# Attention with 16-wide heads: both scores of a turn on the same half, one placing of the maxima, and loops written out

## The chip, the cores and the metric

The kernel runs on one core of a Trainium2 chip. The metric is the device time of one execution in microseconds (us), the median over runs. TensorE (PE in the rows) multiplies, VectorE is DVE, ScalarE is ACT, GpSimd is POOL, SyncE (SP) issues most transfers.

## What is computed

Four layers on 16 sequences of 128 tokens, width 256; each layer is self-attention, cross-attention and a feed-forward part, each followed by a residual and a layer norm. Four of these twelve parts run through one function, `attention16`: the cross-attentions of layers 1, 2 and 3 (stages x1, x2, x3) and the self-attention of layer 3 (stage a3). Cut to what matters:

```python
def attention(x, ctx):                       # 16 heads of 16, 128 queries, 128 keys
    q, k, v = split(x @ Wq), split(ctx @ Wk), split(ctx @ Wv)
    scores = einsum('bhqd,bhkd->bhqk', q, k) / 4   # x1: q, k rotated by position first
    probs = softmax(scores)                  # x2: masked; a3: scores + log(penalty)
    return einsum('bhqk,bhkd->bhqd', probs, v)     # then @ Wo + bo (not in a3)
x = layernorm(x + attention(x, ctx))
```

The penalties of a3 are made in stage ao2, which also adds the outputs of layer 2's experts:

```python
g = sigmoid(h @ Wg + bg)
res = (1 - Zi) * max(1 - Zi - Zj, 0) + Zi * min(1 - Zi + Zj, 1)
scope = clip(126 ** (1 - g) + 2 - abs_ij, 1e-32, 1)
```

## The kernel before

**A turn.** `attention16` handles one sequence in a turn, 16 turns (n = 0 to 15). Queries lie in `qx` and keys in `kx`, [128, 4, 128] each: a row group of 32 rows holds two heads of 16 rows, and of the four slots (c) each keeps one head of every group. Where the other head's rows would be, there is one row that is -1 in `kx` and is to hold the query's maximum in `qx`, so that a product over 32 rows gives the score less the maximum. A half is two of the four row groups (rows 0 to 63, or 64 to 127); 8 of the 16 heads belong to each.

**The steps for a half.** TensorE computes the scores with queries as rows (`score`, L2094, 8 matmuls of 32 x 128 x 128 in float32), VectorE takes the maximum over keys (`maximum`, L2323), TensorE transposes the maxima (`maxima`, L2154), VectorE adds them to their rows of `qx` (`put_maxima`, L2329, four instructions on 64 partitions, 128 elements), TensorE computes the scores again, shifted and with keys as rows (`shifted_score`, L2099, 8 matmuls), ScalarE takes the exponential (L2226). Then come the values (`attend_values`) and the sums of the columns (`attend_sums`), both L2124, VectorE's reciprocal and product (`normalise`, L2380, L2383), the output matrix (`output`, L2146), residual and layer norm (`residual`, `spread`, `scaled`; the root on GpSimd, L1990), and the transposed result goes back to `XT` (`turn_back`).

**Which scores are paired.** The order of a turn is written out by hand. `score_halves` issues two kinds together, matmul by matmul: the scores of half 0 of turn n with the shifted scores of half 1 of turn n - 1, later the scores of half 1 of turn n with the shifted scores of half 0 of the same turn:

```python
for c in range(SLOTS16):
    for j in range(NH):
        done = score(half, j, c, w)
        if shifted:
            last = shifted_score(other, j, c, tw)
```

Here `other = 1 - half`. So four row groups take part in a block. Each half has its own tile `pS[half]` of PSUM, which holds first the scores and then the shifted ones, and its own tile `mx[half]` of maxima. Each float32 matmul is two records in the trace (8 matmuls show as x16), and of one matmul they follow each other in the program.

**The order.** On TensorE in x1 and a3: block 0, turn back, projections of turn n + 1, maxima 0, block 1, (turned keys,) output of n - 2, values of n - 1, maxima 1, sums. In x2 and x3 (`kv`: keys and values were projected in an earlier stage) the output comes between maxima 0 and block 1. VectorE: maximum 0, put 0, maximum 1, residual and spread of n - 2, put 1, scaled, normalise of n - 1; in a3 also `weigh`, the product with the penalties, 1.2 us for each half. The first four and the last two turns are written out, ten run in a hardware loop of two turns. Before a stage's first matmul TensorE waits until GpSimd has cleared `V` and `mx` (L1949). GpSimd also copies the sequence's keys to `kvs` for the values' matmul in x1 and a3.

**Stage ao2.** `add_outputs_and_penalties` loads the experts' biases with 16 small transfers behind a clearing of their tile, all at the stage's start; TensorE waits for them before the first `bias`. The function `least`, three instructions on GpSimd, makes min(1 - Zi + Zj, 1) Zi for groups 0 to 2 of 4, VectorE makes it for the last. VectorE's order is sums 0, 1, 2, penalty 0, sums 3, penalties 1, 2, 3.

## Time and profile before

| | |
|---|---|
| median of 3 runs | 3023.47 us (3021.82 to 3034.4) |
| the profiled execution | 3028.75 us, its span 3026.8 us, granted clock 0.906 of full |
| stage x1, from the first clearing to the last copy to `XT` | 235.05 us |
| stage x2 | 200.48 us |
| stage a3 | 226.03 us |
| stage x3 | 170.38 us |
| stage ao2 | 75.01 us |

Busy over the whole span: TensorE 2443.6 us (81%), VectorE 1523.6 (50%), ScalarE 874.6 (29%), GpSimd 690.0 (23%). These are means over stages with different limits, so each of the five stages is read by itself. Busy TensorE is the time in which at least one matmul is under way, and matmuls overlap.

### The profile page before, as it was taken

Reading aid. Unit: us, or ns where it says so; the run is one execution under the profiler, and the core shown is the slowest. Engines: PE = TensorE matmul, PEld = TensorE weight load, DVE = VectorE, ACT = ScalarE, POOL = GpSimd, SP = SyncE. Lnnn points to the kernel's source line nnn. Section 1 sums busy time; section 2 is a strip of 40 time slices with the busy share of each in tenths; the row PEclk is TensorE's granted clock in tenths of the full one; section 3 lists DMA queues with packets and bytes.
Section 4 is the critical chain, followed back from the end, with each engine's and each line's share of the span. In section 5 each row is a group of like instructions: output and inputs, shape, how many; then the busy total and the mean of one; then the engine's idle time right before and its main releaser. Section 6 shows DMA issues by size and latency. Waiting matters only on the chain. (4 is left out here: it accounts for less than half of the span.)

```text
span 3026.8 us, 55542 instructions
## 1 busy us (share of the span) xinstructions
PE 2443.6 (81%) x20565; PEld 1911.5 (63%) x20565; DVE 1523.6 (50%) x3278; ACT 874.6 (29%) x1558; POOL 690.0 (23%) x1052
## 2 busy tenths in 40 slices
PE   7879998579788799999799878549867757589990
PEld 3857776334567465899688655338556646479990
DVE  3256665775387531111467557541268858721115
ACT  1123333554234211011222244203244435212220
POOL 1932222331133100122112101113221111123331
PEclk8889999889899999999899989769889969889995
DMA  8010000000200000888200020116200000179982
GB/s 324 28 52 1 0 0 6 25 0 1 78 2 0 29 1 0 318 315 315 90 15 0 4 68 0 34 54 183 65 1 1 0 4 1 36 267 323 327 294 85
DMA packets 163394, 253.06 MB, mean 84 GB/s; under 512 B 17744, under 2 KB 124496, under 8 KB 163024
## 3 DMA queue, kind: packets, MB, share of 16 engines
q1 hardware_dynamic: 154064, 230.46, 21.9%
q0 software_dynamic: 9216, 21.06, 2.6%
q8 instruction: 74, 1.21, 0.2%
q14 instruction: 40, 0.33, 0.0%
HBM read 220.36 MB, written 31.13 MB: 83 GB/s over the span
## 5 line engine op out<-in xcount | busy, mean ns | idle before, releaser
L3274 PE MATMUL te_pU<-te_xsT,te_wu 128*128 128x128 f32 x1952 | 236.2, 278 | 1.5 <-DVE te_xsT L3354 1.5
L3274 PEld LDWEIGHTS te_pU<-te_xsT,te_wu 128*128 128x128 f32 x1952 | 233.7, 195 | 5.4 <-issue 2.3
L3295 PE MATMUL te_pY<-te_wd,te_hT 128*128 128x256 f32 x976 | 220.8, 379 | 0.0
L3295 PEld LDWEIGHTS te_pY<-te_wd,te_hT 128*128 128x128 f32 x976 | 180.7, 190 | 22.0
L2094 PE MATMUL x_pS<-x_kx,x_qx 32*128 32x128 f32 x1536 | 120.2, 296 | 62.2 <-issue 34.4
L2323 DVE TENSOR_REDUCE x_mx<-x_pS 128x8 f32<-128x1024 f32 x96 | 117.5, 1224 | 92.4 <-PE x_pS L2094 91.7
L2094 PEld LDWEIGHTS x_pS<-x_kx,x_qx 32*128 32x128 f32 x1536 | 102.9, 199 | 95.8 <-issue 95.8
L2226 ACT ACTIVATE x_Pr<-x_pS 128x1024 f32<-128x1024 f32 x96 | 98.3, 1024 | 161.1 <-PE x_pS L2099 161.1
L1117 PE MATMUL x_pB<-early,x_xlT 128*128 128x384 f32 x384 | 137.5, 502 | 4.7 <-DVE x_qn L1344 3.0
L2329 DVE SCALAR_TENSOR_TENSOR x_qx<-x_pX,place,x_qx 64x128 f32<-64x128 f32 x384 | 109.7, 347 | 23.1 <-PE x_pX L2154 19.7
L2099 PE MATMUL x_pS<-x_qx,x_kx 32*128 32x128 f32 x1536 | 118.3, 294 | 0.7 <-DVE x_qx L2329 0.7
L3315 ACT ACTIVATE te_hT<-te_pU 128x512 f32<-128x512 f32 x78 | 46.6, 597 | 243.2 <-PE te_pU L3274 243.2
L3333 DVE COPY te_ys<-te_pY 128x256 f32<-128x256 f32 x61 | 25.9, 425 | 162.8 <-PE te_pY L3295 162.8
L3328 DVE TENSOR_TENSOR te_hT<-te_pU,te_sg 128x512 f32<-128x512 f32 x44 | 30.4, 692 | 150.4 <-ACT te_sg L3313 150.4
L1117 PEld LDWEIGHTS x_pB<-early,x_xlT 128*128 128x128 f32 x384 | 71.1, 195 | 47.7 <-issue 5.2
L2099 PEld LDWEIGHTS x_pS<-x_qx,x_kx 32*128 32x128 f32 x1536 | 99.4, 196 | 1.7 <-DVE x_qx L2329 1.2
L3313 ACT ACTIVATE te_sg<-te_pG 128x512 f32<-128x512 f32 x44 | 26.3, 597 | 252.4 <-PE te_pG L3274 252.4
L3330 DVE COPY te_xsT<-te_pT 128x256 f32<-128x256 f32 x61 | 25.7, 421 | 135.2 <-PE te_pT L3268 135.2
L1990 POOL TENSOR_TENSOR x_rstd<-x_ve,mhalf 128x1 f32<-128x1 f32 x48 | 26.4, 551 | 292.0 <-DVE x_ve L2370 292.0
L3274 PE MATMUL te_pG<-te_xsT,te_wg 128*128 128x128 f32 x704 | 87.1, 278 | 0.0
L2036 PE MATMUL x_pq<-XT,early 128*128 (+1 forms) x512 | 75.4, 302 | 12.4 <-POOL x_mx L1949 12.4
L2380 DVE RECIPROCAL x_R<-x_pO 128x256 f32<-128x256 f32 x48 | 84.3, 1757 | 1.4
(625 smaller groups left out, 5757.8 us busy)
## 6 DMA issues: line engine op xcount, KB each, us to landing
te_wu<-in_L_ffn_w_upT SPq DMA_DIRECT2D x39, 1024.0 KB, 5.4
te_wd<-in_L_ffn_w_downT SPq DMA_DIRECT2D x39, 1024.0 KB, 5.6
te_wu<-in_L_ffn_up SPq DMA_DIRECT2D x22, 1024.0 KB, 4.8
te_wg<-in_L_ffn_gate SPq DMA_DIRECT2D x22, 1024.0 KB, 6.9
te_wd<-in_L_ffn_down SPq DMA_DIRECT2D x22, 1024.0 KB, 7.6
moe_first<-in_L_ffn_W SPq DMA_DIRECT2D x8, 1024.0 KB, 8.7
ao_got<-ys_slots SPq DMA_DIRECT2D x12, 512.0 KB, 6.1
xs_slots<-zeros SPq DMA_DIRECT2D x1, 5120.0 KB, 23.5
```

The source lines that it names most:

```text
L1117: ins = pe.matmul(pB[:, n, 0:HALF], xlT[t][:, src + k, :], w[:, k, bass.ts(n, HALF)], start=(k == 0), stop=(k == KD - 1))
L2036: ins = pe.matmul(out[:, t, :], ws[t // KD][:, k, bass.ts(t % KD, P)], src[:, k, bass.ts(b, P)], start=(k == 0), stop=(k == KD - 1))
L2094: return pe.matmul(pS[half][:, j, c, :], qx[w][g, c, :], kx[w][g, c, :], start=mask is None, stop=mask is None or c == SLOTS16 - 1)
L2099: return pe.matmul(pS[half][:, j, c, :], kx[w][g, c, :], qx[w][g, c, :], start=mask is None, stop=mask is None or c == SLOTS16 - 1)
L2226: ins = act.activation(Pr[w][half][:], pS[half][:], ACT.Exp, scale=SCALE)
L2323: dve.tensor_reduce(out, pS[half][:], AX.X, ALU.max).then_inc(mx_ready[half], 1)
L2329: ins = dve.scalar_tensor_tensor(out=qx[w][g, c, :], in0=pX[g, 2 + half, :], scalar=place[g, c:c + 1], in1=qx[w][g, c, :], op0=ALU.mult, o ...
L2380: dve.reciprocal(R[:], pO[:, 1, :, :]).then_inc(o_inverted, 1)
L3274: ins = pe.matmul(out[g][:, m, :], w[:, k, bass.ts(PER * g + m, P)], xsT[:, k, :], start=(k == 0), stop=(k == KD - 1))
L3295: ins = pe.matmul(pY[u][:, 0, :], hT[:, k, :], wd[u][:, k, :], start=(k == 0), stop=(k == KH - 1))
L3315: act.activation(hT[:, PER * g:PER * (g + 1), :], pU[g][:], act_fn).then_inc(h_done, 1)
L3328: dve.tensor_tensor(hT[:, PER * g:PER * (g + 1), :], pU[g][:], sg[g][:], ALU.mult).then_inc(h_done, 1)
```

## The change

- **Pairing.** `scores(n, half)` issues the scores of that half of turn n into one tile `pR` and the shifted scores of the same half of turn n - 1 into another, `pT`. Both are used for half 0 and again for half 1, so block 1 waits for the maximum and the exponential of block 0.
- **Maxima.** Both halves write one tile `mx` [128, 2, 128]; TensorE makes two transposes in one go after block 1; `put_maxima` is two instructions on 128 partitions, 256 elements each. The constants `others`, `minus` and `place` have two columns, so that `key` is two instructions (in a3 still four).
- **Depth.** Work of earlier turns is one turn later than before: the output is of turn n - 3 (a3: n - 4), turning back of n - 4 (n - 5); in a3 the values are those of n - 2 (`LAG` = 2). `qx` and `kx` have four buffers, `V` three (a3: four), `oT` two.
- **Loops.** All turns are written out; the `hold` increments go. TensorE no longer waits for the clearing; ScalarE does for `V` and VectorE for `mx`. `kvs` and its copies go.
- **ao2.** The biases' tile is kept from earlier: cleared by a transfer at the start of x2, loaded by 16 small transfers in the experts' stage behind the second expert's weights. `least` goes, VectorE does its two instructions in every group, in the order sums 0, sums 1, penalty 0, sums 2, penalty 1, sums 3, penalties 2, 3. TensorE begins with bias 0; the last group's keys are made after the first logits.

```diff
@@ attention16
+        LAG = 2 if penalty is not None else 1
+        TURNS = range(-1, NB + LAG + 3)
-        pS = [s.ps(f"pS{i}", [P, NH, SLOTS16, P]) for i in range(2)]
+        pR, pT = s.ps("pR", [P, NH, SLOTS16, P]), s.ps("pT", [P, NH, SLOTS16, P])
@@ tensor
+            def scores(n, half):
+                if mask is not None:
+                    if live(n):
+                        masks(pR, mask[0], n)
+                    if live(n - 1):
+                        masks(pT, mask[1], n - 1)
                 for c in range(SLOTS16):
                     for j in range(NH):
-                        done = score(half, j, c, w)
-                        if shifted:
-                            last = shifted_score(other, j, c, tw)
+                        if live(n):
+                            done = score(half, j, c, n)
+                        if live(n - 1):
+                            last = shifted_score(half, j, c, n - 1)
+            for n in TURNS:
+                if live(n):
+                    since(pe, q_stored, n)
+                    since(pe, k_stored, n)
+                    since(pe, mx_ready[1], n - 1)
+                if live(n - 1):
+                    since(pe, m_stored, n - 1)
+                    since(pe, e_done[1], n - 2)
+                scores(n, 0)
+                if rope and live(n + 1):
+                    projections(n + 1)
+                if live(n - LAG - 3):
+                    turn_back(n - LAG - 3)
+                if own and live(n - LAG - 2):
+                    output(n - LAG - 2, n)
+                if kv and live(n + 1):
+                    projections(n + 1)
+                if live(n):
+                    since(pe, mx_ready[0], n)
+                if live(n - 1):
+                    since(pe, e_done[0], n - 1)
+                scores(n, 1)
+                if own and live(n + 1):
+                    projections(n + 1)
+                if rope and live(n + 1):
                     turned_keys(n + 1)
+                if not own and live(n - LAG - 2):
+                    output(n - LAG - 2, n + 1)
+                if not kv and live(n):
+                    maxima(n)
+                if live(n - LAG):
+                    attend_values(n - LAG)
+                if kv and live(n):
+                    maxima(n)
+                if live(n - LAG):
+                    attend_sums(n - LAG)
@@ vector
+            def put_maxima(b):
+                since(dve, m_ready, b)
+                for i in range(PAIR):
+                    here = qx[b % 4][:, KD * i:KD * (i + 1), :]
+                    ins = dve.scalar_tensor_tensor(out=here, in0=pX[:, 2:4, :], scalar=place[:, i:i + 1], in1=here,
+                                                   op0=ALU.mult, op1=ALU.add)
+                ins.then_inc(m_stored, 1)
+            for n in TURNS:
+                if live(n):
+                    maximum(n, 0)
+                if own and live(n - LAG - 2):
+                    residual(n - LAG - 2)
+                if rope and live(n + 1):
+                    rotate(n + 1, q_ready, bqc, bqc2, rq, q_turned, q_summed)
+                if live(n - LAG - 1):
+                    normalise(n - LAG - 1)
+                if live(n):
+                    maximum(n, 1)
+                if rope and live(n + 1):
+                    rotate(n + 1, k_ready, bkc, bkc2, rk, k_turned, k_summed)
+                if not own and live(n - LAG - 2):
+                    residual(n - LAG - 2)
+                if live(n):
+                    put_maxima(n)
+                if live(n - LAG - 2):
+                    spread(n - LAG - 2)
+                if penalty is not None and live(n - 1):
+                    weigh(n - 1, 0)
+                    weigh(n - 1, 1)
+                if live(n - LAG - 2):
+                    scaled(n - LAG - 2)
@@ stage ao2
-            core.x3.wait(pe)
-            kv.make_keys(pe, 0)
             pe.wait_ge(wT_stored, 1)
-            pe.wait_ge(loaded, 16 * NG * G)
+            pe.wait_ge(lists.biases_loaded, 16 * NG * G)
             bias(0)
-            for g in range(1, NG):
+            core.x3.wait(pe)
+            for g in range(NG - 1):
                 kv.make_keys(pe, g)
```

## Rows read from the trace of the kernel before

**Rows 1.** The page, its first line: the whole span
```profile
span 3026.8 us, 55542 instructions
```

**Rows 2.** Windows by stage: x1, x2, a3, x3, ao2 (busy us of each engine, clock)
```profile
797.69:1032.74 235.05, 180.66 (x2752) 152.93 (x2752) 167.78 (x400) 83.42 (x161) 67.26 (x116) 0.95 0.08 26
1736.73:1937.21 200.48, 157.20 (x2432) 107.56 (x2432) 133.63 (x272) 80.23 (x160) 27.53 (x52) 0.93 0.09 27
2227.77:2453.80 226.03, 162.94 (x2464) 131.23 (x2464) 170.90 (x309) 90.98 (x192) 41.59 (x85) 0.84 0.00 1
2456.62:2627.00 170.38, 124.69 (x2304) 98.62 (x2304) 131.79 (x272) 80.34 (x160) 27.51 (x52) 0.91 0.01 2
2151.31:2226.32 75.01, 60.59 (x225) 36.34 (x225) 47.54 (x87) 32.35 (x49) 22.61 (x18) 0.89 0.10 30
```

**Rows 3.** The same, steady turns: 11 of x1, 10 of x2, 12 of a3, 12 of x3
```profile
866.46:1009.22 142.76, 115.86 (x1885) 98.31 (x1883) 114.78 (x277) 56.40 (x112) 44.96 (x76) 1.00 0.00 1
1794.58:1904.06 109.48, 90.93 (x1521) 62.92 (x1522) 83.34 (x171) 49.89 (x100) 16.39 (x30) 1.00 0.00 1
2268.78:2418.91 150.13, 113.99 (x1849) 91.48 (x1850) 126.53 (x228) 68.06 (x144) 28.21 (x59) 0.91 0.00 1
2489.40:2599.57 110.17, 85.95 (x1736) 68.16 (x1734) 98.43 (x205) 60.01 (x121) 19.65 (x36) 1.00 0.00 1
```

**Rows 4.** Groups of stage x1 (count, busy us, mean ns, idle before)
```profile
L2323 DVE TENSOR_REDUCE x_mx<-x_pS 128x8 f32<-128x1024 f32 x32 | 39.1, 1223 | 28.7 <-PE x_pS L2094 28.6
...
L2329 DVE SCALAR_TENSOR_TENSOR x_qx<-x_pX,place,x_qx 64x128 f32<-64x128 f32 x128 | 36.5, 346 | 1.2 <-PE x_pX L2154 0.6
```

**Rows 5.** Timeline of TensorE, first turn of x1 (start us, us)
```profile
810.29 1.16 PE L2094 MATMUL x_pS<-x_kx,x_qx 32*128 32x128 f32 x16 [3.75 <-issue]
811.38 3.56 PE L2036 MATMUL x_pq<-XT,early 128*128 128x128 f32 x16
...
817.30 0.34 PE L2094 MATMUL x_pS<-x_kx,x_qx 32*128 32x128 f32 x1 [1.25 <-issue]
817.31 0.37 PE L2099 MATMUL x_pS<-x_qx,x_kx 32*128 32x128 f32 x1
817.31 0.37 PE L2094 MATMUL x_pS<-x_kx,x_qx 32*128 32x128 f32 x1
817.32 0.37 PE L2099 MATMUL x_pS<-x_qx,x_kx 32*128 32x128 f32 x1
...
818.40 2.05 PE L2036 MATMUL x_pq<-CT,early 128*128 128x128 f32 x16
```

**Rows 6.** Timeline of all engines, one turn of x3
```profile
2545.78 0.33 PE L2154 MATMUL x_pX<-ident,x_mx 128*128 128x128 f32 x1 [0.36 <-DVE x_mx L2323]
...
2546.04 1.08 PE L2124 MATMUL x_pO<-x_Pr,ones_half 128*32 128x128 f32 x32
2546.15 1.17 DVE L2329 SCALAR_TENSOR_TENSOR x_qx<-x_pX,place,x_qx 64x128 f32<-64x128 f32 x4
...
2547.35 1.76 DVE L2380 RECIPROCAL x_R<-x_pO 128x256 f32<-128x256 f32 x1
...
2547.57 0.34 PE L2094 MATMUL x_pS<-x_kx,x_qx 32*128 32x128 f32 x1 [0.45 <-DVE x_qx L2329]
...
2548.82 1.02 ACT L2226 ACTIVATE x_Pr<-x_pS 128x1024 f32<-128x1024 f32 x1 [1.07 <-PE x_pS L2099]
...
2550.92 1.04 PE L2146 MATMUL x_pk<-early,x_oT 128*128 128x256 f32 x4
```

**Rows 7.** Timeline of TensorE, start of x3
```profile
2458.00 2.05 PE L2036 MATMUL x_pq<-XT,early 128*128 128x128 f32 x8 [4.69 <-POOL x_mx L1949]
```

**Rows 8.** Timeline of stage ao2, three places
```profile
2158.97 0.66 PE L4043 MATMUL ao_pb<-ao_biases,ao_WT 32*128 32x512 f32 x1 [1.32 <-DMA ao_biases<-in_L_ffn_b]
...
2167.62 1.38 DVE L4140 TENSOR_SCALAR ao_xn<-ao_r,ao_mv,ao_rstd 128x256 f32<-128x256 f32 x4 [1.17 <-POOL ao_rstd L4011]
...
2194.73 2.47 DVE L4140 TENSOR_SCALAR ao_xn<-ao_r,ao_mv,ao_rstd 128x256 f32<-128x256 f32 x4 [1.14 <-POOL ao_rstd L4011]
```

More of the change, by code:

```diff
@@ L2038, in project, with value @@
                 return ins
-            def value():
+            def value(b):
                 for k in range(KD):
-                    ins = pe.matmul(pv, kvs[:, k, :], wv[:, k, :], start=(k == 0), stop=(k == KD - 1))
-                return ins
-            def y_free(b):
-                if not (isinstance(b, int) and b <= 1):
-                    pe.wait_ge(y_used, b - 1)
-            def projections(b, first=False):
+                    ins = pe.matmul(pv, KV[:, k, bass.ts(b, P)], wv[:, k, :], start=(k == 0), stop=(k == KD - 1))
+                ins.then_inc(v_ready, 1)
@@ L2079, in turned_keys, with masks @@
             def turned_keys(b):
-                pe.wait_ge(q_turned, b + 1)
-                hold(pe, core)
+                since(pe, q_turned, b)
                 project(pq, (wk, wk2), KV, b).then_inc(k_ready, 1)
-            def masks(half, table, b):
+            def masks(out, table, b):
                 for j in range(NH):
-                    pe.matmul(pS[half][:, j, :, :], core.identb[:],
+                    pe.matmul(out[:, j, :, :], core.identb[:],
                               table[:, b, :].unsqueeze(1).to_broadcast([P, SLOTS16, P]), start=True, stop=False)
@@ L2136, in attend_sums @@
-            def attend_sums(w):
-                columns(1, lambda h, i: ones_half[:, i, :], w).then_inc(o_ready, 1)
-            def output(b, ahead):
-                pe.wait_ge(oT_ready, b + 2)
-                pe.wait_ge(y_used, b + 2)
-                if not kv and ahead:
-                    pe.wait_ge(v_copied if rope else k_stored, b + ahead)
+                                            Pr[b % 2][g // NH][:, g % NH, KD * (1 - i) + t, :], start=(i == 0),
+                                            stop=(i == PAIR - 1))
@@ L2192, in _ @@
-            projections(0, first=True)
-            if rope:
-                turned_keys(0)
-            every_turn(pe, turn)
-            LAST = NB - 1
-            pe.wait_ge(m_stored[1], NB)
-            if mask is not None:
-                masks(1, mask[1], LAST)
-            for c in range(SLOTS16):
-                for j in range(NH):
-                    ins = shifted_score(1, j, c, 1)
-            ins.then_inc(t_ready[1], 1)
-            turn_back(LAST - 2)
-            output(LAST - 1, 0)
@@ L2298, in _ @@
-            query(0, 0)
-            value(0, 0)
-            key(0, 0)
-            every_turn(act, turn)
-            exponentials(NB - 1, 1, 1)
-            for b in range(NB - 3, NB):
-                turn_back(b)
+            for n in TURNS:
+                if live(n - 1):
+                    exponentials(n - 1, 0)
+                if live(n - LAG - 3):
+                    turn_back(n - LAG - 3)
+                if rope and live(n + 1):
+                    value(n + 1)
+                if not own and live(n + 1):
+                    query(n + 1)
+                if live(n - 1):
+                    exponentials(n - 1, 1)
+                if own and live(n + 1):
+                    query(n + 1)
+                    value(n + 1)
+                if live(n + 1):
+                    key(n + 1)
+                if kv and live(n + 1):
+                    value(n + 1)
@@ L2411, in _ @@
-            if rope:
-                turn_queries(0, first=True)
-                turn_keys(0, first=True)
-            every_turn(dve, turn)
-            residual(NB - 2)
-            spread(NB - 2)
-            if penalty is not None:
-                weigh(NB - 1, 1, 1)
-            scaled(NB - 2)
-            normalise(NB - 1)
-            residual(NB - 1)
-            spread(NB - 1)
-            scaled(NB - 1)
+                since(dve, y_ready, b - 2)
+                dve.tensor_tensor(oT[b % 2][:], pO[:, 0, :, :], R[:], ALU.mult).then_inc(oT_ready, 1)
@@ L3945, in _, with add_outputs_and_penalties @@
                 steps.end()
-def add_outputs_and_penalties(core, a, name, W, b2, got, keys, values, weight):
+def add_outputs_and_penalties(core, name, W, lists, keys, values, weight):
     BASE = float(np.log(P - 2.0))
@@ L4089, in _ @@
             act.copy(WT[:], pw[:, 0, :]).then_inc(wT_stored, 1)
[L4090 removed]
+            for g in range(NG - 1):
                 kv.store_keys(act, g)
@@ L4160, in _ @@
             sums(0)
-            sums(1)
-            sums(2)
-            penalty(0)
-            sums(3)
-            penalty(1)
-            penalty(2)
-            penalty(3)
+            for g in range(1, NG):
+                sums(g)
+                penalty(g - 1)
+            penalty(NG - 1)
 def expert_weights(core, keep, name):
@@ L4205, in layer2 @@
         list_experts(core, a, "te2", ACT.Gelu_apprx_tanh, lists, after=[core.x3])
-        add_outputs_and_penalties(core, a, "ao2", W, "L2_ffn_b2", lists.outputs, core.keys3, spare, core.pen.weight)
+        add_outputs_and_penalties(core, "ao2", W, lists, core.keys3, spare, core.pen.weight)
 def layer3(core, a, spare):
```

509 lines of the change are left out of this document (177 added, 332 removed).

## The prediction

> **What bounds the kernel now.** I read the page for the whole span [rows 1], cut it by stage [rows 2], and then took from each of the four attention stages a stretch of steady turns [rows 3]. The reader is to see there that no engine is full. A turn takes 142.76 / 11 = 12.98 us in x1, 109.48 / 10 = 10.95 in x2, 150.13 / 12 = 12.51 in a3 and 110.17 / 12 = 9.18 in x3. VectorE is busy for 10.4, 8.3, 10.5 and 8.2 us of it, TensorE for 10.5, 9.1, 9.5 and 7.2. Neither has much room, and the rest is waits of one for the other: VectorE waits for the scores before its maximum 28.7 us in x1 [rows 4], TensorE for the maxima put in their place [rows 6]. So a change can gain by VectorE's work, or by unlocking the chain, and it loses where it adds to TensorE's.
>
> **The block of scores.** This is the term on which the sum hangs. In x1's first turn a block is alone, without shifted scores: 16 records (8 matmuls) on two row groups, and the next matmul starts 811.38 - 810.29 = 1.09 us later. The following block has 32 records on four row groups and takes 818.40 - 817.30 = 1.10 us [rows 5]. Twice the work cost nothing, because it fell on other row groups: in both cases a row group gets 8 records, so a record costs about 0.11 us of its group, and about 0.2 us are start and switch. The new pairing puts the scores and the shifted scores of the same half together, so 32 records fall on two row groups: 16 x 0.11 + 0.2 = about 1.98 us, 0.88 us more per block, 1.76 us per turn. The bounds: 1.10 us, if something other than the row group (the PSUM bank, of which four are still used) sets the pace, and 2.84 us, if the two groups overlap only where the program goes from one to the other. In that case the 32 records have 24 gaps of 0.11 us, since four records in a row now belong to one group. I take 1.98, since the four first records start at 817.30 to 817.32 on four groups [rows 5], although the second record of each matmul stands between them in the program: a blocked group doesn't hold the others.
>
> The Trainium skill, in TensorE: Matmul & The Clock Gate, Part 3, says the reverse, that matmuls start strictly in program order and only weight loads are pulled ahead. By it the block would be the 2.84 us; the trace of before speaks against it, in the same four records.
>
> **VectorE's part.** `put_maxima` has 8 instructions of 0.346 us per turn [rows 4], 1.17 us busy for each half [rows 6]. The new ones have 256 elements on all partitions. The reduction of 1,024 elements takes 1.223 us and this one of 128 takes 0.346 [rows 4], so an element costs about 0.98 ns and one with 256 takes about 0.47; two take 0.9 us. That frees 1.4 us per turn. Bounds for the two: 0.7 us (each as short as now) and 1.4 (each as two of the old).
>
> **x3, by its new chain.** Block 0 starts at 0 and ends at 1.98. The maximum starts 0.1 later and takes 1.22, and TensorE starts 0.25 us after VectorE's last instruction (put from 2546.15 to 2547.32, block at 2547.57 [rows 6]): block 1 from 3.6 to 5.6. Projections and turning back lie under the maximum, VectorE's reciprocal (1.76 us [rows 6]) and product under block 1. Then the exponential of block 1 starts 0.15 later and takes 1.02 [rows 6]; the output matrix (1.04 us) lies under it. The values of turn n - 1 need that exponential and stand ahead of the transposes in the program: from 6.9 to 7.9 (as the sums, 1.08 us with its tail [rows 6]). Two transposes reach VectorE at 8.4 (one takes 0.37 from 2545.78 to 2546.15 [rows 6]), put ends at 9.3, and the next block 0 starts at 9.6. The sums of the columns lie under put. VectorE's spread, a wait for GpSimd's root, which nothing on VectorE covers in this order, and scaled lie under the next block 0; without that cover the wait would be paid in each turn. So 9.6 us against 9.18: the chain was to be loosened, but the wider blocks stand twice in it. 16 x 0.4 = 6.5 us lost.
>
> **x2** adds the mask matmuls, 10.95 - 9.18 = 1.77 us per turn at present, and they stand in the chain as before: 11.4 against 10.95, 7 us lost.
>
> **x1.** TensorE has 10.5 us per turn at full clock [rows 3], and 1.76 more make 12.3. VectorE has 10.4 - 1.4 = 9.0, and the path from the turned keys over GpSimd and ScalarE has its two instructions of `key` in place of four. I take TensorE as the bound, as the busier one: 12.3 against 12.98, 16 x 0.7 = 11 us gained.
>
> **a3.** Here VectorE also weighs, so the freed work and the second turn of lag count. VectorE needs 10.5 - 1.4 = 9.1 us [rows 3]; in the new order it waits before put for the transposes, which stand behind the projections of the next turn (16 records of 0.11 us and 4 of twice the width, 2.6 us); normalise and the rest cover some 1.5 us of it, which leaves an estimated 1.1 us, and 0.4 us of handovers: 10.6. TensorE has 9.5 us at a clock of 0.91 and gets 1.8 more, 11.3, or less if the clock rises with the load. I take 11.0 against 12.51: 16 x 1.5 = 24 us gained.
>
> **Starts and ends.** TensorE now starts without GpSimd's clearing, on which x3's first matmul waited [rows 7]: 1.4 us per stage. The end of a stage is longer by about 3 us, since the last blocks come one after the other through single tiles and the last two turns' layer norms queue with one turn more of depth. 6 us lost in four stages. The loops written out and `kvs` I leave at nothing: branches and copies lie beside the longer work, and without that cover they'd be tenths of a microsecond per turn. More instructions to fetch are priced by no row; the transfer engines' share is 0.00 in the steady turns [rows 3], so there is room for them.
>
> **ao2.** TensorE waits for the biases until 2158.97, 7.7 us into the stage [rows 2, 8]. With them there, bias 0 starts at about 2152, and the first layer norm begins when the experts' outputs land, about 5.5 us earlier. The 16 transfers move to the experts' queue ahead of a wait for a whole expert, so they delay nothing. Without `least` beside it the same instructions take 1.38 us, with it 2.47 [rows 8], so VectorE gets 1.5 us more of work per group and loses as much of slowing down. The last group's keys, too, go behind the first turning back, which takes some 3 us from TensorE's path ahead of it. A group then needs sums and penalty on VectorE one after the other, as it does at present from group 2 on. So the stage ends at least the 5.5 us earlier, at most these, the keys' 3 and twice 2 us of slowing down (12.5); I take 10.
>
> **The sum.** x1 -11, x2 +7, x3 +6.5, a3 -24, starts and ends +6, ao2 -10: about -26 us. From the profiled execution's 3028.75 us that is 3003; it lies 5.3 us above the median of the runs, 3023.47, so I predict 2998 us for the median.
>
> **Rivals.**
> - *Matmuls in strict order* (the other side). Each block costs 2.84 us, 0.86 more, twice in the chain of each of 64 turns: +110 us, 3108 us. It decides against the change from 1.98 + 0.2 us per block on. For it: four records of one group in a row are new, and no row shows such a block. Against it: [rows 5]. 12%.
> - *Exposed waits.* The chain of a turn now has single tiles between TensorE, VectorE and ScalarE, and if each of the handovers costs 0.05 to 0.1 us more than I have read, a turn is 0.35 us longer: 22 us, 3020. For it: x2 and x3 are chains without slack. 20%.
> - *The row group isn't the pace.* Blocks stay at 1.1 us; then x1 has 10.6, x3 7.8, x2 9.7 and a3 10.5, another 92 us: 2906 us. Against it: a record costs 0.11 us of its group in both blocks of [rows 5]. 4%.
> - *My forecast* as it stands, 2975 to 3012 us: 60%. A larger gain in a3 and ao2 (put cheaper, the clock up), 2960 to 2975: 4%.
>
> **How the numbers follow.** About 0.5%, 15 us, is what a measurement of this kernel can tell from no change: 3008 and 3038.6 are the borders. Of my own case about 54 in 100 lie below, with both faster cases 62; another 2 for waits that turn out small. Within: 6 of my own, and 17 of the exposed waits. Slower: the strict order and what is left of the waits, 13. Range: 2962 to 3035 us; it leaves out strict order and the unpaced blocks.
>
> **What would show it.** In the profile after: a block of 32 records takes 1.98 us to the next matmul (2.84 or 1.1 would be the rivals); put is two instructions of 0.47 us; steady turns of 12.3, 11.4, 11.0 and 9.6 us; VectorE idle before put in a3; bias 0 at the start of ao2, that stage at 65 us. The prediction is wrong above all if blocks are slower, and next if a3's turn stays near 12.5 us.

## The result, and the profile after

The changed kernel takes 3048.59 us (median of 5 runs, 3041.17 to 3054.53) against 3029.54 for the kernel before (5 runs beside it): 1.0066 times as long, 95% interval 1.0041 to 1.0091. It is slower by 19 us, 0.7%, where 2998 us and a gain of 26 us were predicted, and it lies outside the range. (The kernel before had 3023.47 us when the prediction was made, and 3029.54 beside the changed one.) The profiled execution has 25.8 us more than that of [rows 1], 53,590 instructions and a granted clock of 0.894.

Windows of the profile after, by stage: x1, x2, a3, x3, ao2 (columns as in [rows 2]).

```profile
795.55:1027.92 232.37, 212.20 (x2752) 190.45 (x2752) 143.23 (x304) 76.61 (x129) 62.10 (x100) 0.93 0.09 27
1729.81:1941.85 212.04, 193.12 (x2432) 142.47 (x2432) 110.06 (x176) 70.76 (x128) 27.77 (x52) 0.90 0.09 29
2225.11:2474.07 248.96, 213.00 (x2464) 190.47 (x2464) 146.35 (x212) 91.19 (x192) 46.41 (x70) 0.74 0.01 1
2475.83:2652.70 176.87, 158.20 (x2304) 132.31 (x2304) 110.09 (x176) 70.78 (x128) 27.77 (x52) 0.90 0.02 3
2155.60:2224.80 69.20, 60.31 (x225) 36.31 (x225) 46.28 (x93) 32.12 (x49) 9.41 (x8) 0.91 0.09 31
```

The same for steady turns: 11 of x1, 10 of x2, 10 of a3, 12 of x3.

```profile
864.51:1001.61 137.10, 134.49 (x1894) 122.19 (x1893) 97.82 (x209) 51.60 (x88) 41.57 (x67) 1.00 0.01 2
1798.27:1910.66 112.39, 109.81 (x1522) 82.32 (x1521) 68.48 (x110) 43.95 (x80) 16.26 (x30) 1.00 0.01 2
2301.59:2438.62 137.03, 129.94 (x1542) 117.14 (x1541) 89.44 (x131) 56.71 (x120) 29.37 (x41) 0.75 0.01 2
2516.45:2627.97 111.52, 108.20 (x1728) 91.07 (x1727) 82.19 (x132) 52.52 (x95) 19.35 (x36) 1.00 0.01 2
```

Against [rows 3]: x1 12.98 to 12.46 us a turn (12.3 forecast), x2 10.95 to 11.24 (11.4), x3 9.18 to 9.29 (9.6). a3 goes from 12.51 to 13.70 instead of 11.0, and there alone the clock column is not 1.00 but 0.75; it was 0.91 before. VectorE has lost its work as forecast, 89.44 / 10 = 8.9 us a turn. So the stage that was to bring the gain is limited by TensorE's clock.

Groups of stage x1, as in [rows 4].

```profile
L2252 DVE TENSOR_REDUCE x_mx<-x_pR 128x8 f32<-128x1024 f32 x32 | 39.1, 1222 | 33.1 <-PE x_pR L2042 33.1
L2259 DVE SCALAR_TENSOR_TENSOR x_qx<-x_pX,place,x_qx 128x256 f32<-128x256 f32 x32 | 13.8, 473 | 0.0
```

One turn of x3 on the timeline, start, and the rows that follow the blocks.

```profile
2542.28 0.50 PE L2042 MATMUL x_pR<-x_kx,x_qx 32*128 32x128 f32 x4 [0.16 <-issue]
2542.57 0.42 PE L2047 MATMUL x_pT<-x_qx,x_kx 32*128 32x128 f32 x4
...
2544.33 0.44 PE L2112 MATMUL x_pX<-ident,x_xn 128*128 128x128 f32 x2
...
2545.63 0.50 PE L2042 MATMUL x_pR<-x_kx,x_qx 32*128 32x128 f32 x4
...
2547.71 1.13 PE L2095 MATMUL x_pk<-early,x_oT 128*128 128x256 f32 x4
```

A block takes 2544.33 - 2542.28 = 2.05 us and 2547.71 - 2545.63 = 2.08 to the next matmul, where it was 1.10 in [rows 5].

One turn of a3, all engines.

```profile
2344.05 0.50 PE L2042 MATMUL a_pR<-a_kx,a_qx 32*128 32x128 f32 x4 [0.71 <-DVE a_mx L2252]
...
2345.24 0.82 PE L2047 MATMUL a_pT<-a_qx,a_kx 32*128 32x128 f32 x4
...
2346.85 2.08 PE L2000 MATMUL a_pq<-XT,early 128*128 128x128 f32 x8
2346.87 1.22 DVE L2252 TENSOR_REDUCE a_mx<-a_pR 128x8 f32<-128x1024 f32 x1
...
2352.11 0.38 PE L2105 MATMUL a_pX<-ident,a_mx 128*128 128x128 f32 x2
...
2352.53 0.88 DVE L2259 SCALAR_TENSOR_TENSOR a_qx<-a_pX,place,a_qx 128x256 f32<-128x256 f32 x2 [4.45 <-PE a_pX L2105]
```

The four records that take 0.42 us in x3 take 0.82 here within the same block. Eight records of projections take 2.08 us; at full clock they take 1.16 (experiment 6). VectorE waits 4.45 us for the transposes that stand behind them. Windows of 1 us over the same turn put a number to it (last three columns: granted clock, share of the transfer engines, GB/s).

```profile
2344.00:2345.00 1.00, 0.94 (x15) 0.98 (x17) 0.86 (x3) 0.17 (x1) 0.00 (x0) 1.00 0.00 0
2345.00:2346.00 1.00, 1.00 (x16) 1.00 (x14) 1.00 (x1) 0.00 (x0) 0.00 (x0) 0.62 0.00 0
...
2347.00:2348.00 1.00, 1.00 (x5) 1.00 (x6) 1.00 (x1) 1.00 (x1) 0.00 (x0) 0.50 0.00 0
...
2351.00:2352.00 1.00, 1.00 (x7) 1.00 (x6) 0.00 (x0) 1.00 (x4) 0.00 (x0) 0.50 0.00 0
2352.00:2353.00 1.00, 1.00 (x26) 0.83 (x29) 0.47 (x2) 1.00 (x4) 0.48 (x1) 0.96 0.00 0
```

From 2.4 GHz (1.00) the clock falls to 1.2 (0.50) at about 2345.2, while TensorE is at work without a break, 1.2 us after the end of a pause of 0.71, and it is back at 2352.1, just when the projections are done. Each of the ten steady turns goes that way: TensorE is busy for 12.99 us, idle for 0.71, and some 7 of the 13.70 us pass at the lower clock.

Stage ao2, as in [rows 8].

```profile
2156.49 3.77 PE L3939 MATMUL ao_pb<-moe_biases,ao_WT 32*128 32x512 f32 x4 [0.35 <-ACT ao_WT L3983]
...
2160.30 1.22 DVE L4016 TENSOR_TENSOR ao_r<-X,ao_pb 128x1024 f32<-128x1024 f32 x1 [4.32 <-PE ao_pb L3939]
...
2166.12 1.38 DVE L4032 TENSOR_SCALAR ao_xn<-ao_r,ao_mv,ao_rstd 128x256 f32<-128x256 f32 x4 [1.17 <-POOL ao_rstd L3920]
...
2195.60 1.38 DVE L4032 TENSOR_SCALAR ao_xn<-ao_r,ao_mv,ao_rstd 128x256 f32<-128x256 f32 x4 [1.12 <-POOL ao_rstd L3920]
```

The biases are there, 2.47 us have become 1.38, and the first layer norm comes 10.5 us into the stage (16.3 before). By the same 5.8 us the stage is shorter, not by 10. (Experiment 12 asks how much of that is the edit's.)

### The profile page after: what moved, and what is told of

Read it like the earlier page. It is cut to its first block and busy times, and to the rows that moved or that the text cites. A ratio compares the mean times of both kernels' runs of the same rounds, so it can differ in the third digit from the quotient of the medians.

```text
span 3052.6 us, 53590 instructions
## 1 busy us (share of the span) xinstructions
PE 2592.3 (85%) x20565; PEld 2075.3 (68%) x20565; DVE 1428.0 (47%) x2899; ACT 848.5 (28%) x1462; POOL 675.4 (22%) x1011
## 5 line engine op out<-in xcount | busy, mean ns | idle before, releaser
L2042 PE MATMUL x_pR<-x_kx,x_qx 32*128 32x128 f32 x1536 | 188.5, 305 | 18.5 <-ACT x_kx L2200 13.3
L2042 PEld LDWEIGHTS x_pR<-x_kx,x_qx 32*128 32x128 f32 x1536 | 154.6, 200 | 48.2 <-issue 43.7
L2252 DVE TENSOR_REDUCE x_mx<-x_pR 128x8 f32<-128x1024 f32 x96 | 117.6, 1225 | 141.0 <-PE x_pR L2042 140.5
L2047 PE MATMUL x_pT<-x_qx,x_kx 32*128 32x128 f32 x1536 | 176.1, 281 | 1.2 <-ACT x_Pr L2167 1.2
L2167 ACT ACTIVATE x_Pr<-x_pT 128x1024 f32<-128x1024 f32 x96 | 98.2, 1023 | 255.6 <-PE x_pT L2047 255.4
L2047 PEld LDWEIGHTS x_pT<-x_qx,x_kx 32*128 32x128 f32 x1536 | 151.9, 196 | 3.0 <-ACT x_Pr L2167 1.7
L3239 DVE COPY te_ys<-te_pY 128x256 f32<-128x256 f32 x61 | 25.9, 425 | 162.8 <-PE te_pY L3201 162.8
L2042 PE MATMUL a_pR<-a_kx,a_qx 32*128 32x128 f32 x512 | 70.8, 328 | 20.8 <-DVE a_mx L2252 14.0
L2000 PE MATMUL x_pq<-XT,early 128*128 128x128 f32 x512 | 80.6, 315 | 5.2 <-PEq L284 3.0
```

The lines of the kernel that those rows point to most:

```text
L2000: ins = pe.matmul(out[:, t, :], ws[t // KD][:, k, bass.ts(t % KD, P)], src[:, k, bass.ts(b, P)], start=(k == 0), stop=(k == KD - 1))
L2042: return pe.matmul(pR[:, j, c, :], qx[b % 4][g, c, :], kx[b % 4][g, c, :], start=mask is None, stop=mask is None or c == SLOTS16 - 1)
L2047: return pe.matmul(pT[:, j, c, :], kx[b % 4][g, c, :], qx[b % 4][g, c, :], start=mask is None, stop=mask is None or c == SLOTS16 - 1)
L2167: ins = act.activation(Pr[b % 2][half][:], pT[:], ACT.Exp, scale=SCALE)
L2252: dve.tensor_reduce(out, pR[:].rearrange("p j (i t) n -> p (j i) t n", i=PAIR), AX.X, ALU.max).then_inc(mx_ready[half], 1)
```

## The experiments

Each was timed beside the kernel before on the same chip, and its ratio is against that (3028 to 3029 us there). In these terms the changed kernel has 1.0066. Turns are counted from one maximum of half 0 to the next, and a trace is of one execution.

**1. The pairing alone put back.** Four row groups in a block again, the rest as changed:

```diff
-                            last = shifted_score(half, j, c, n - 1)
+                            last = shifted_score(1 - half, j, c, n - 1)
```

with the semaphores, the two exponentials and the two `weigh` in the order that follows.

> The changed kernel with one part undone: a block holds the scores of one half of turn n and the shifted scores of the other half of turn n - 1 (half 1 in block 0, half 0 in block 1), so that four row groups take part again; the exponentials and the two products with the penalties go in that order too. Everything else stays changed. Theory: the row group is the pace, a block takes 1.1 us instead of 2.05 to 2.08, and where the blocks stand in the chain a turn is 1.8 to 1.9 us shorter: x3 9.3 to 7.5 us, x2 11.2 to 9.4, x1 12.5 to 11.0 (VectorE's 9 us and its waits take over), 60 to 90 us in the whole: 2960 to 2990 us. Rival: with the wide blocks gone TensorE is idle for longer and its granted clock falls in these stages, as it does in a3 of the changed kernel; then a block takes 2 us again by its clock and the kernel stays above 3020 us.

2902.03 us, ratio 0.958 (0.9567 to 0.9593). Steady turns of x1, x2, a3, x3 (11, 13, 11, 11):

```profile
855.29:972.44 117.15, 113.22 (x1893) 100.86 (x1894) 96.77 (x210) 50.39 (x88) 41.64 (x67) 1.00 0.01 2
1726.33:1848.47 122.14, 116.24 (x1969) 80.08 (x1970) 87.34 (x138) 56.09 (x102) 19.55 (x36) 1.00 0.01 2
2209.77:2315.20 105.43, 88.39 (x1690) 75.66 (x1690) 97.00 (x144) 63.46 (x132) 31.64 (x42) 1.00 0.01 2
2391.84:2475.77 83.93, 78.97 (x1585) 62.05 (x1586) 72.98 (x122) 48.41 (x88) 18.04 (x34) 1.00 0.01 3
```

The turns are 10.65, 9.40, 9.58 and 7.63 us: less than in the changed kernel by 1.8, 1.8, 4.1 and 1.7. In three stages that is the 1.76 us of the prediction. In a3 it is 2.3 more, and the clock there is 1.00. The pairing costs 147 us in all (0.0486 of 3028.6), where I had expected 60 to 90. It isn't all the blocks' own: in the traces fifteen turns are shorter by 30.2, 30.9 and 28.6 us in x1, x2 and x3, some 90 us, and by 56.6 in a3. Against a3's turn of 10.81 at full clock (experiment 6), the blocks account for 1.2 us a turn there, some 20 us; so about 110 of the 147 us come from the blocks and about 37, an estimate from these rows, from a3's clock. The rest of the change is worth 127 us: this version beats both kernels.

**2 to 4. Is it a3, and is it the clock?** Stage a3 run by the attention function of before; in a3, the next turn's projections moved ahead of block 1; in a3, eight idle transposes in the pause ahead of block 1:

```diff
-    attention16(core, a, "a3", core.a3, ...)
+    attention16_old(core, a, "a3", core.a3, ...)
```

```diff
-                if kv and live(n + 1):
+                if (kv or own) and live(n + 1):
                     projections(n + 1)
...
-                if own and live(n + 1):
-                    projections(n + 1)
```

```diff
+                if own and live(n):
+                    since(pe, v_copied, n)
+                    for i in range(8):
+                        pe.transpose(pq[:, 0, :], core.ident[:], core.ident[:])
                 if live(n):
                     since(pe, mx_ready[0], n)
```

> The changed kernel, with stage a3 alone run by the attention function of the kernel before (its own constants with four columns beside the new ones). Theory: a3's loss of 23 us is the whole of the difference and more, and comes from inside that stage: 3025 us, a3 back at 226 us with turns of 12.5. Rival: the turns of a3 are slow by what stands ahead of the stage (the clock in the stages before it, the place of code); then a3 stays near 249 us and the kernel at 3048.

> The changed kernel, in a3 alone the next turn's projections move from behind block 1 to between the output and block 1, where TensorE waits 0.7 us for the maximum; the maxima's transposes then follow block 1 directly. Theory (the transposes wait for projections at half clock, which fill 5.3 us between block 1 and the transposes, and VectorE waits 4.45 us before put): block 1 comes 1.3 to 2 us later, the wait before put shrinks to under 1 us, and a turn takes 11.5 to 12.3 us instead of 13.7: a3 is 20 to 30 us shorter, 3020 to 3028 us. Rival (the length of the turn is given by the number of columns TensorE has to do at the low clock, wherever they stand): the wait moves to the maximum before block 1 and the turn stays at 13.3 to 13.7 us, 3042 to 3048 us.

> The changed kernel, in a3 alone 8 more transposes of the identity into the idle tile of the queries stand ahead of the wait for the maximum of block 1, where TensorE is idle for 0.71 us in each turn. They do nothing for the result. Theory (the 0.7 us without work are what lets the clock fall in block 1): the granted clock of a3 goes from 0.75 to near 1.0, block 1 takes 2.15 us and not 2.85, the projections 2.6 us and not 5.3, the turn falls to 11.0 to 11.5 us, the kernel to 3005 to 3015 us. Rival (the clock falls by the kind of work, blocks on two row groups and products of 32 columns, and not by idle time): clock and turn stay at 0.75 and 13.7 us or get 0.2 us worse, 3048 to 3052 us.

The old a3 gives 3032.52 us, ratio 1.0011 (1.0 to 1.0022): 17 us of the loss is in that stage's code, and what stood ahead of it didn't make it slow. In the trace the stage takes 228.2 us (226.03 before, 248.96 in the changed kernel), with turns of 12.3 to 13.4. That is 2 of the 7.5 us above my 3025; the rest wasn't followed.

The moved projections give 3046.06 us, 1.0051 (1.0038 to 1.0065), nearly nothing. From the third on the turns are between 11.7 and 13.7 us, the last five 13.63; VectorE waits less before put (0.56 us), and instead 2.9 us before the second maximum. The rival's figures came, but its reason isn't what the trace shows. The clock in these last turns is 0.87 and not 0.75, so the slow stretch is half as long; what keeps the turn long is that TensorE now pauses for 2.2 us of it, busy for 11.46, where it paused for 0.71. At full clock this order takes 11.7 and 11.8 us (two turns), longer than the 10.8 of the changed kernel's order. So the move gains at the low clock what it loses in waits.

The fillers give 3021.82 us, 0.9967 (0.9955 to 0.998), 30 us less than the changed kernel. Windows of 11 steady turns, and three rows of one:

```profile
2284.91:2405.15 120.24, 116.61 (x1782) 106.46 (x1781) 101.00 (x143) 62.14 (x131) 32.09 (x43) 1.00 0.01 2
```

```profile
2354.96 1.03 PE L2006 MATMUL a_pq<-early,XT 128*128 128x256 f32 x4
...
2357.14 0.88 DVE L2263 SCALAR_TENSOR_TENSOR a_qx<-a_pX,place,a_qx 128x256 f32<-128x256 f32 x2 [1.32 <-PE a_pX L2105]
...
2361.86 1.04 PE L2135 MATMUL a_pq<-ident 128*128 128x128 f32 x8
```

Here is the clock of 1.00, the wait before put of 1.32 us where I had estimated 1.1, and a turn of 120.24 / 11 = 10.93 us: the 11.0 of the prediction, to be had at full clock only. The time stayed above the expected 3005 to 3015 because the first three turns of the stage took 14.6, 16.5 and 15.1 us, at a clock of 0.60 to 0.66 and with the added work (12.1, 13.8 and 13.8 in the changed kernel).

**5. Which work holds the clock?** The same pause filled by four matmuls of 32 rows, a quarter of the array.

```diff
-                    for i in range(8):
-                        pe.transpose(pq[:, 0, :], core.ident[:], core.ident[:])
+                    for i in range(4):
+                        pe.matmul(pq[:, 0, :], core.ident[0:ROWS, :], core.ident[0:ROWS, :], start=True, stop=True)
```

> As the run with fillers in a3, but the 8 transposes on 128 rows are replaced by 4 matmuls of 32 rows by 128 by 128 on one row group, 8 records of about 0.11 us, so that the same 0.7 to 0.9 us ahead of block 1 is filled by work on a quarter of the array. They do nothing for the result. Theory (any instruction that keeps TensorE from pausing will do): the granted clock of a3 goes to 1.00 as with the wide fillers, turns of 10.9 us, the kernel at 3020 us. Rival (it counts how much of the array is at work: the wide blocks use two of four row groups, while the kernel with the other pairing, which is idle for longer, stands at 1.00): the clock stays at 0.75 to 0.85 and the turn at 13.0 to 13.9 us, 3043 to 3052 us.

3026.25 us, 0.9988 (0.9978 to 0.9998). The first five turns take 10.8 to 13.8 us, the last ten 10.82 at a clock of 1.00:

```profile
2300.00:2402.00 102.00, 98.75 (x1543) 89.97 (x1543) 86.02 (x124) 54.37 (x118) 28.50 (x38) 1.00 0.01 2
```

So work on a quarter of the array does as well as work on the whole. Whether it helps by filling the pause or by moving what stands behind it, these two runs don't tell. The pause alone doesn't decide: in experiment 1 TensorE pauses for 0.83 and 0.48 us in each turn of a3, and the clock stays at 1.00.

**6. ao2 put back**, on the changed kernel: the `add_outputs_and_penalties` of before and its transfers.

```diff
-            lists.request_biases(sp, a["L2_ffn_b2"])
-        add_outputs_and_penalties(core, "ao2", W, lists, core.keys3, spare, core.pen.weight)
+        add_outputs_and_penalties(core, a, "ao2", W, "L2_ffn_b2", lists.outputs, core.keys3, spare, core.pen.weight)
```

> The changed kernel, with stage ao2 and the biases' transfers put back as they were (16 transfers at the stage's start behind GpSimd's clearing, the minimum on GpSimd for groups 0 to 2, the order of before). Theory: the stage is 6 us longer again, 75 us instead of 69.3, and nothing else moves: 3055 us. Rival (the stage's gain is given back in a3, which then starts from other clocks, or the early transfers slow the experts' stage by the 1 to 4 us by which ao2 started later): 3047 to 3050 us, with ao2 starting earlier.

3050.22 us, 1.0055 (1.0029 to 1.0082), single runs from 3031 to 3063. That was too wide for ao2, but the trace gave something else. One of the slow turns of a3, and the first two of the last three of the same stage; below them the eight records of projections from the first fast one:

```profile
2325.35:2339.05 13.70, 12.99 (x156) 11.71 (x155) 9.00 (x13) 5.66 (x12) 2.94 (x5) 0.75 0.01 2
2394.55:2405.37 10.82, 9.79 (x156) 8.84 (x155) 9.18 (x14) 5.66 (x12) 2.97 (x5) 1.00 0.02 4
2405.37:2416.18 10.81, 9.78 (x156) 8.82 (x155) 9.17 (x13) 5.66 (x12) 2.95 (x5) 1.00 0.01 2
```

```profile
2397.96 1.16 PE L2000 MATMUL a_pq<-XT,early 128*128 128x128 f32 x8
```

The same 156 records take 13.70 us at a clock of 0.75 and 10.8 at 1.00, without any filler. The turns before the switch drifted: 13.81, 13.92, 14.03. What drifted can be seen in the first 2 us behind the pause of 0.7 us, in a slow turn, in the last two slow turns and in the first fast one:

```profile
2326.70:2328.70 2.00, 2.00 (x25) 2.00 (x27) 1.85 (x3) 0.12 (x1) 0.00 (x0) 0.69 0.03 8
2367.95:2369.95 2.00, 2.00 (x22) 2.00 (x23) 1.85 (x3) 0.12 (x1) 0.00 (x0) 0.62 0.00 0
2381.87:2383.87 2.00, 2.00 (x19) 2.00 (x21) 1.85 (x3) 0.12 (x1) 0.00 (x0) 0.55 0.03 8
2395.90:2397.90 2.00, 2.00 (x32) 1.94 (x32) 1.86 (x3) 0.12 (x1) 0.00 (x0) 1.00 0.04 8
```

The clock is 1.00 up to the fall and 0.50 behind it, so a mean of 0.69 puts the fall 0.8 us behind the pause; then it came 0.5 and 0.2 us behind it, and in the next turn not at all. In the steady turns of the changed kernel it comes 1.4 us behind the pause at first and 0.9 in the last ones, and the stage ends before it gets there.

**7. Fillers in five turns only.** From that came a sharper question: does the stage hold whichever pattern it has got into?

```diff
-                if own and live(n):
+                if own and live(n) and n <= 4:
```

> The changed kernel, with the 8 idle transposes ahead of block 1 of a3 in the turns 0 to 4 alone; from turn 5 on every instruction is that of the changed kernel. In the run with the old ao2 the last three turns of a3 took 10.81 us at a clock of 1.00, with the instructions unchanged, after twelve of 13.7 to 14.0. Theory (the same turn can run in two patterns: one of 13.7 us in which the clock falls to half once in every turn, and one of 10.8 us at full clock; which of them holds depends on how it begins): from turn 5 on the turns stay at 10.8 us, a3 is about 25 us shorter, 3020 to 3028 us. Rival (the pause of 0.7 us pulls the clock down anew in each turn, whatever came before): from turn 6 on 13.7 us again, 3040 to 3048 us.

3034.2 us, 1.0015 (0.9999 to 1.0031), single runs from 3015 to 3044. In the profiled execution the turns from 5 on are 10.8 us, with three of 12.3 to 14.0 between them, and the clock from turn 3 on is 0.95. The theory holds in part: the fast pattern outlasts its fillers and even comes back after a fall, but it isn't safe; the gain over the changed kernel is half of what lasting fillers give (0.0051 against 0.0099).

**8 and 9. How far does a blocked row group hold the others?** The matmuls of a block in another order: group by group, and strictly by turns.

```diff
-                for c in range(SLOTS16):
-                    for j in range(NH):
+                for j in range(NH):
+                    for c in range(SLOTS16):
```

```diff
                 for c in range(SLOTS16):
                     for j in range(NH):
                         if live(n):
                             done = score(half, j, c, n)
+                    for j in range(NH):
                         if live(n - 1):
                             last = shifted_score(half, j, c, n - 1)
```

> The changed kernel, in each block the order of the matmuls alone is different: first all 8 on the first of the half's two row groups (scores and shifted scores by turns), then all 8 on the second. The same matmuls, row groups and tiles. Theory as the prediction put it (a record costs its own row group 0.11 us and a blocked group doesn't hold the others, however far apart they stand in the program): a block stays at 2.05 us and the kernel at 3048 us. Rival (TensorE looks only so far ahead, or not at all: records start in the order of the program, and two groups overlap only where the program goes from one to the other): 32 records one after the other, 3.5 us a block, 1.5 us more twice in each of 64 turns, up to 190 us, 3230 us.

> The changed kernel, in each block the order alone is different: score on the first group, score on the second, shifted score on the first, shifted score on the second, where the changed kernel has four records of one group in a row. Theory (the row group is the pace): a block stays at 2.05 us, the kernel at 3045 to 3050 us. Rival (the order matters a little, four records in a row of one group leave the other without work): a block of 1.9 us or less, 0.15 us twice in 64 turns, 3030 us.

Group by group gives 3377.16 us, 1.1143 (1.1126 to 1.116). A block of x2, its start, its middle and what follows:

```profile
2001.40 0.48 PE L2042 MATMUL x_pR<-x_kx,x_qx 32*128 32x128 f32 x2
2001.72 0.38 PE L2047 MATMUL x_pT<-x_qx,x_kx 32*128 32x128 f32 x2
...
2002.84 0.49 PE L2042 MATMUL x_pR<-x_kx,x_qx 32*128 32x128 f32 x4
...
2004.82 0.44 PE L2112 MATMUL x_pX<-ident,x_xn 128*128 128x128 f32 x2
```

The block takes 3.42 us: the records follow each other 0.11 us apart, two in 0.22. Only at the middle, where the last four of one group and the first four of the next meet, do the groups overlap (x4 for x2, from 2002.84 on). My theory falls and the rival holds: a waiting record does hold what stands well behind it. How far is shown by that start: the second group's first record goes when only three records of the first are still waiting ahead of it in the program, and not earlier. In the order of the changed kernel it's three too, and little is lost there: 2.05 us against the 1.98 of experiment 9. The 1.37 us more per block are 175 us in 64 turns; the total is 326 us more than the changed kernel (0.1077 of 3029), and the clock probably has a part in the rest (0.851 over the span against 0.894).

By turns gives 3012.62 us, 0.9937 (0.9922 to 0.9952). A block of x3 takes 2564.67 - 2562.69 = 1.98 us:

```profile
2562.69 0.49 PE L2042 MATMUL x_pR<-x_kx,x_qx 32*128 32x128 f32 x4 [0.16 <-issue]
2562.99 0.42 PE L2047 MATMUL x_pT<-x_qx,x_kx 32*128 32x128 f32 x4
...
2564.67 0.44 PE L2113 MATMUL x_pX<-ident,x_xn 128*128 128x128 f32 x2
```

Turns are 12.29 in x1, 11.02 in x2, 9.09 in x3, 0.17 to 0.22 us less, 9 us in three stages. And a3 gets out of the slow pattern after five turns: ten of 10.67 us. A change of 0.1 us per block brought 39 us; 31 of them are a3's turns (205.42 to 174.8 in the traces), which went from one pattern to the other.

**10 and 11. What the two other parts are worth**, on the kernel of experiment 1: the maxima placed by 8 instructions of 64 rows; and a3 with one turn of lag.

```diff
-                for i in range(PAIR):
-                    here = qx[b % 4][:, KD * i:KD * (i + 1), :]
+                for h in range(2):
+                    g = slice(P // 2 * h, P // 2 * (h + 1))
+                    for c in range(SLOTS16):
+                        here = qx[b % 4][g, c, :]
...
```

```diff
-        LAG = 2 if penalty is not None else 1
+        LAG = 1
```

> The kernel with the other pairing, with the placing of the maxima as 8 instructions of 64 rows and 128 elements instead of 2 of 128 rows and 256; nothing else is different. Theory: 8 take 2.35 us (twice the 1.17 us of before) and 2 take 0.88, the placing stands in the chain of each turn, so a turn is 1.4 to 1.5 us longer in all four stages: 64 x 1.45 = 93 us, 2990 to 3000 us. Rival (part of it lies under the values and sums of TensorE, 2 us, which block 0 waits for anyway in x1 and a3): 0.3 to 0.8 us per turn, 2920 to 2950 us.

> The kernel with the other pairing, in a3 with values one turn behind the scores instead of two (LAG 1), as in the other stages. Theory (the second turn of lag hides VectorE's product with the penalties, 2.35 us): TensorE waits for the product ahead of the values in each turn, a turn is 1.5 to 2.5 us longer than 9.58 us, the drain one turn (about 5 us) shorter: 2920 to 2935 us. Rival (the product lies beside the sums and block 0, and a deeper pipeline only lengthens the drain): 2895 to 2900 us.

Eight instructions: 3013.95 us, 0.9953 (0.9935 to 0.9971), 113 us more. Turns are 11.97, 10.82 and 9.09 in x1, x2 and x3: 1.3 to 1.5 us longer each, as expected, 19 to 22 us a stage. a3 is back in mixed turns of 11.3 to 13.2 at 0.85, 36 us longer in fifteen turns, and that is most of the part above 93. The placing stands in the chain with its whole length. One turn of lag: 2957.28 us, 0.9762 (0.9748 to 0.9777), 55 us more, above the 2920 to 2935 that I expected. Its a3 turn is 14.1 us and not 11 to 12:

```profile
2309.29 2.35 DVE L2265 TENSOR_TENSOR a_Pr<-a_Pr,early 128x1024 f32<-128x1024 f32 x2
2311.70 1.94 PE L2073 MATMUL a_pO<-a_Pr,a_V 128*32 128x128 f32 x32 [3.52 <-DVE a_Pr L2265]
2313.41 1.55 PE L2073 MATMUL a_pO<-a_Pr,ones_half 128*32 128x128 f32 x32
```

TensorE waits 3.52 us for the product, and pays again behind the wait: values and sums take 3.2 us, the greater part of it at a clock of 0.5, where they take 1.9 in experiment 1.

**12. ao2 once more**, the edit of experiment 6 on the kernel of experiment 1, where a3 doesn't stray.

> The kernel with the other pairing, with stage ao2 and the biases' transfers put back as they were. With the changed kernel as base the same edit gave 3050.2 against 3048.6 us, with a spread of 30 us that came from a3's clock; here a3 runs at a clock of 1.00 in each of its steady turns, so that the stage can be weighed. Theory (the late biases and the slowed layer norms cost what the two profiles of ao2 differ by, 71.5 against 68.9 us from the first copy of the weights to a3's first matmul): 2.6 us, 2904.5 us. Rival (the 6 us by which the stage of before is longer than that of the changed kernel are all of this edit's making): 2908 us. Second rival (the early transfers cost the experts' stage as much as they bring): 2902 us.

2902.2 us, 0.9594 (0.9576 to 0.9612), against 2902.03: no difference. From the first copy of the weights to a3's first matmul the stage takes 71.6 us with the old ao2 (clock 0.91) and 70.3 with the new (clock 0.85). The second rival was right as to the time; whether the experts' stage pays for it, a difference of 1 us can't say.

## Why the prediction was wrong

By its own terms, from the profiled executions; a stage's turns run from its first to its sixteenth maximum of half 0:

| term | predicted | measured |
|---|---|---|
| turns of x1 | -11 | 193.65 - 197.73 = -4.1 |
| turns of x2 | +7 | 173.51 - 168.39 = +5.1 |
| turns of x3 | +6.5 | 145.75 - 139.33 = +6.4 |
| turns of a3 | -24 | 205.42 - 188.98 = +16.4 |
| starts and ends | +6 | starts -7.7, ends +22.1: +14.4 |
| ao2 | -10 | -5.8 |
| the remainder, stages that the change leaves alone | 0 | -6.6 |
| sum | -26 | +25.8 |

- **The step that failed is a3's turn.** "TensorE has 9.5 us at a clock of 0.91 and gets 1.8 more, 11.3, or less if the clock rises with the load. I take 11.0 against 12.51". The turn at full clock was right, 10.93 us with fillers and 10.8 without them in the fast pattern; there VectorE's path is the bound (9.2 us busy, 1.2 of wait before put, the 10.6 of the prediction), and TensorE is busy for 9.8. The clock was not right: it went from 0.91 to 0.75, with one fall in every steady turn, for some 7 us of 13.7. That adds 3.2 us of busy time to TensorE (12.99 against 9.79) and makes it the bound. a3's turns are 40 of the 52 us between forecast and result. The row with 0.91 already stood in [rows 3], and I let it count in one direction only.
- **The block** was right: 1.98 predicted, 2.05 to 2.08 measured, 1.98 with alternating groups. Two of my reasons need mending. Strict order doesn't give 2.84 here, but "a blocked group doesn't hold the others" is true over a few records only (experiment 8). The Trainium skill's strict order (TensorE: Matmul & The Clock Gate, Part 3, The mechanism) thus doesn't agree with the 2.05 us of the changed kernel, and agrees with the 3.42 us of groups that stand far apart, but for the seam.
- **VectorE's part** was right: 2 x 0.473 = 0.95 us against 0.9, 0.88 on the timeline.
- **x2 and x3** were right in sign: 11.24 and 9.29 us a turn against 11.4 and 9.6. That x3's +6.4 meets the forecast of +6.5 is luck. Its steady loss is 0.1 us a turn and not 0.4; the other 4.9 us lie in its first two turns (10.81 and 14.13 us, before 10.75 and 9.32), at clocks of 0.50 and 0.55, a term that I didn't have. In four other traces with the same x3 its fifteen turns take 151.2 us, 12 more than before.
- **x1** has 12.46 against 12.3. TensorE is busy for 134.49 of 137.10 us and is the bound as predicted. Its first four turns are 15.0, 13.95, 14.0 and 13.6 us, at clocks of 0.73 to 0.90 and 6.7 over the steady ones, where before they were 3.1 over. In five other traces with the same x1 its fifteen turns take 189.5 us, 8 less than before; so 4 of the 7 us missing to -11 are of this execution.
- **Starts and ends.** Starts gained 1.4 to 2.4 us in each stage (1.4 predicted). Ends are 2.8, 8.8, 8.2 and 2.3 us longer for 3 in each. a3's has the second turn of lag in it. x2's is 31.2 us here and in one other trace with the same x2, and 25.9 to 26.4 in five more, so it isn't of the change's making alone.
- **ao2.** The first layer norm is 5.8 us earlier, as the 5.5 predicted, and that is all; what I added to it, up to 10, for the keys and the slowed instructions didn't come. Nor is all of the 5.8 the edit's: with the old ao2 the stage was 2.5 and 1.3 us longer in two pairs of runs (71.5 against 69.0, 71.6 against 70.3), where [rows 2] has it at a clock of 0.89 and these old ones at 0.91. On the kernel of experiment 1 the edit changed nothing in the whole time.
- **The rivals.** Neither strict order nor exposed waits nor an unpaced block came. The last paragraph, "What would show it", named a3's turn second, with 12.5 us, and gave no mechanism by which it could get longer than before. The missing rival was: more work on TensorE in a stage whose clock is already not full.

What stays open: what picks the pattern at a stage's start, and why. In the changed kernel the fall comes 0.9 to 1.4 us after a pause of 0.71, but the same pause is there in the fast turns of experiment 6, and 0.83 us in experiment 1. That the pattern ends when the fall has drifted up to the pause is seen once, in experiment 6, and wasn't tested. It wasn't tried whether a filler elsewhere in the turn does as well.

## What to carry to other kernels

Work packed on row groups costs by the fullest group, so pair what goes together over all groups; here that is about 110 us by the blocks themselves, and 147 of 3049 with what it does to a3's clock. In the program let groups alternate: here a group passed three waiting records of another and no more. And read the clock column per stage before pricing anything on TensorE: a3 was at 0.91 before, and with 1.8 us more work the same turn had two lengths, 13.70 and 10.81 us. An edit of 0.1 us moved it from one to the other, so such a stage has to be priced at both.

## What the hardware showed unexpectedly

- The granted clock can fall to 1.2 GHz once per turn while TensorE is busy for 95% of the time (129.94 of 137.03 us), and stay at 2.4 GHz while it is busy for 84% (88.39 of 105.43 us, experiment 1). The Trainium skill describes a clock that swings with the loop where short pauses recur (TensorE: Matmul & The Clock Gate, A second HAM failure mode: psum-queue depth-cycling). The turns of 13.70 us, with a pause of 0.71 and a clock of 0.75, agree with it; but the same instructions, with the same pause, also run at 10.81 us with the clock at 1.00.
- Single runs of one kernel differ more with such a stage: 3031 to 3063 us and 3015 to 3044 in experiments 6 and 7, against 2899 to 2907 in experiment 1, where a3 holds its clock. That the stage makes the difference is likely but not shown, since one run of each has a trace.
- Two matmuls of one row group and two of another overlap fully (8 records in 0.45 us); sixteen records of one ahead of sixteen of the other don't (8 in 0.9), but for the four on each side of the seam.
